# Second expert site: rows scattered to expert slots by chunks inside the linear attention, tiles loaded by plain transfers

## The chip, the cores and the metric

One core of one Trainium2 chip runs one kernel. The metric is device microseconds (us) of one launch. Five engines run their own instruction streams and meet at semaphores: PE (matrix products, into PSUM banks), ACT (activations), DVE (vector operations), POOL (vector operations and the issue of indirect DMAs) and SP (here only the issue of plain DMAs and the waits before them).

## The reference, cut to what matters

2048 tokens (8 sequences of 256) of 128 channels, float32, go through: a local-attention network of two layers, an attention with distance decay, the same local-attention network again, a mixture of experts, a linear attention, and the same mixture of experts again. The change is in the last two. The mixture is computed twice, each time on the normalised rows:

```python
x = x + 0.5 * _L1_ffn_ref(_layernorm(x), ...)          # first expert site
x = x + _L1_attn_ref(_layernorm(x), ...)               # linear attention, causal within 512 tokens
x = x + 0.5 * _L1_ffn_ref(_layernorm(x), ...)          # second expert site
# _L1_ffn_ref: D = 128, E = 12 experts, HR = 384, HS = 256, TAU = 1.5
ys = _geglu(xf @ Ws1 + bs1) @ Ws2 + bs2                # shared expert, all rows
logits = (xf @ Wr + br) / TAU
top_val, top_idx = jax.lax.top_k(logits, 2)            # two experts for each row
top_w = jax.nn.softmax(top_val)
yr = sum over the two picks of top_w * (_geglu(xf @ We1[e] + be1[e]) @ We2[e] + be2[e])
return ys + yr
```

## The kernel before, in words

**Tiles.** P = 128 rows are a tile, NT = 16 tiles are all rows, CT = 4 tiles are a chunk, NCH = 4 chunks. X holds the stream, U its normalised rows, uT those transposed. Two picks for each of 2048 rows are 4096 pairs. Sorted by expert and padded to whole tiles they fill at most NXT = 32 + 12 = 44 expert tiles of 128 rows, and the kernel always runs 44. Each stage below has its own stream on each engine (`la_pe`, `mx_dve` and so on), written out by hand, and semaphores are the only other order.

**Stages in order.** Local attention (site 0), decay attention, local attention (site 1), first expert site (`mx_*`, k0 = 0), linear attention (`la_*`), second expert site (`mx_*`, k0 = 1), final sum (`fin_*`). Before the decay attention, after it and around the linear attention stands `phase_end` (L313 to L319): each of PE, ACT, DVE and POOL executes a drain (L315) and then waits for the drains of the other three. SP does not take part.

**Linear attention.** The loop of `la_pe` over i handles chunk i at several depths: `out_proj(i-1)`, `x_turned(i-2)` (transposes of the newly normalised U, L2338), `sums(i)`, `scores(i+1)`, `o_turn(i)` and `logits(i-3)`, the router's product (L2345), whose result for all 16 tiles lies in one bank and is announced once. `la_dve` runs `gated`, `masked`, `result`, `features`, `divided` and `normed` (L2461, makes U) in that order, and `la_pool` computes the power of the variance for each chunk (L2554, L2556).

**Routing, in `mx_dve`.** Both sites do the same, for all 16 tiles at once after the phase end: scaled logits, the two largest and their indices, one-hot masks, weights by a power on POOL (L2193). PE counts rows by expert (`counts`). DVE forms prefix sums, the expert of each of the 44 tiles (`tef`, written as whole numbers to `te` by POOL, L2197), and a place for each pair. One-hot rings (24 of 32 by DVE at L2070, 8 by POOL at L2202) and 32 small products of PE (L1822) invert the places into two tables, `inv_u[0]` (which row each place reads) and `inv_u[1]` (where each place's result goes). Beside it PE and ACT compute the hidden layer of the shared expert (L1786, L1913).

**The expert loop.** For tile n: POOL gathers 128 rows of `u_rows` (a copy of U in DRAM, stored by SP at L2229) by `inv_u[0]` into one of XG = 8 buffers (L2182). PE transposes them (L1833), ACT copies that to xT (L1921), PE multiplies by We1 of the expert (12 instructions, L1845), ACT and DVE form the gated product (L1929, L2105), PE multiplies by We2 (6 instructions, L1859), ACT copies (L1936) and POOL scatters 128 rows to `y_rows` by `inv_u[1]` (L2188). POOL's order is gather(n), scatter(n - 12). SP loads We1 (384 KB) for each tile into one of four buffers once the first product of tile n - 4 has been issued and is done (L2236). It first reads the expert's number from `te` into a register (`expert`, L1777: a TENSOR_LOAD, a FUSED_REGOPS, a SEQ_ASSERT). The product of tile n+1 and the transposition of tile n+2 alternate in `group`. After the last scatter SP loads `y_rows` back, and DVE, ACT and POOL add to X.

Of the kernel before, what the change touches and what calls it, by code (L numbers as in the profile page):

```python
# [16 lines left out]
P = 128  # L17
# [23 lines left out]

V_BE1, V_BS1, V_B1, V_LG, V_LB, V_QKVB, V_LQKVB, V_LGATE, V_LNG, V_LNB, V_N = (
# [11 lines left out]
r_tab h_ld n_gps n_gate n_kps n_k n_neg n_exp n_kf n_qps n_qf n_vps n_v n_att n_am n_num n_den n_rec n_o  # L54
# [68 lines left out]
def build(nc, a, out):  # L123
    with ExitStack() as ctx:
# [177 lines left out]
        ndr = sb("ndr", [P, 2, CT])  # L302

        u_rows = nc.dram_tensor("u_rows", [NT * P, D], F32, kind="Internal").ap()
        y_rows = nc.dram_tensor("y_rows", [2 * NT * P + NXT * P, D], F32, kind="Internal").ap()
# [107 lines left out]
        def constants_pool(pool):  # L415
            pool.memset(ones[:, :], 1.0)
            pool.memset(wts[:, :, E:E + 1], 1.0)
            pool.memset(wts[:, :, E + 1:32], 0.0)
            pool.memset(ebase[:, :], float(np.e))
# [1327 lines left out]
        def sh_up(g):  # L1747
            return B[1 + 2 * g], B[2 + 2 * g]
# [21 lines left out]

        LD_X = (s.ld_x0, s.ld_x1, s.ld_x2, s.ld_x3, s.ld_x4, s.ld_x5, s.ld_x6, s.ld_x7)

# [6 lines left out]
        def mx_pe(pe, k0):  # L1779
            kc, base = k0 * NCH, k0 * NXT  # L1780

            def up(c, g):
                if c:
                    pe.wait_ge(s.s_a, 2 * (kc + c - 1) + g + 1)
                for half in range(2):
                    m = pe.matmul(sh_up(g)[half][:, :], ws1[:, (2 * half + g) * P:(2 * half + g + 1) * P],  # L1786
# [31 lines left out]
            def ring(m):  # L1818
                pe.wait_ge(s.inv_b, k0 * oh_dve(2 * NT) + oh_dve(m + 1))
                if oh_pool(m + 1):  # L1820
# [7 lines left out]
            def x_turn(i, o, q):  # L1828
                n, buf = 8 * i + 4 * o + q, 4 * o + q
                pe.wait_ge(LD_X[buf], 16 * (x_loads(k0, buf) + i + 1))  # L1830
# [47 lines left out]

            up(0, 0)
            up(0, 1)  # L1880
            up(1, 0)
            counts()
# [3 lines left out]
            weights_turn()  # L1886
# [5 lines left out]
            pe.wait_ge(s.r_pool, r_pools(k0) + 2)  # L1892
            pe.wait_ge(s.r_tab, 2 * k0 + 1)
            x_turn(0, 0, 0)
            x_turn(0, 0, 1)
            for i in range(OCT):
                group(i, 0)
                group(i, 1)
# [9 lines left out]
        def mx_act(act, k0):  # L1908
            kc, base = k0 * NCH, k0 * NXT

            def hidden(c, g):
                act.wait_ge(s.s_up, 2 * (kc + c) + g + 1)
                act.activation(acts[:, c, g, :], sh_up(g)[1][:, :], ACT.Gelu, bias=vec[:, V_BS1 + 2 + g:V_BS1 + 3 + g])  # L1913
                act.activation(sh_a[:, c, g, :], sh_up(g)[0][:, :], ACT.Identity, bias=vec[:, V_BS1 + g:V_BS1 + g + 1])\
# [17 lines left out]
            def y_out(n):  # L1932
                act.wait_ge(s.x_dn, base + n + 1)
                if n + k0 * NXT > 3:
                    act.wait_ge((s.st_y0, s.st_y1, s.st_y2, s.st_y3)[n % 4], 16 * (NXG * k0 + n // 4))
# [3 lines left out]
            for c in range(NCH):  # L1939
                for g in range(2):  # L1940
                    hidden(c, g)
                if c == 2:
                    act.wait_ge(s.r_wps, k0 + 1)
                    act.activation(wT[:, :], W_BANK[:, :], ACT.Copy).then_inc(s.r_wT, 1)
            act.wait_ge(s.r_pool, r_pools(k0) + 2)
            x_out(0)
            x_out(1)
            for n in range(NXT + 2):
# [7 lines left out]
        R_PLACES = 34  # L1956
        R_STEPS = 43
        R_TILES = 27

        def mx_dve(dve, k0, coef):  # L1960
            kc, base = k0 * NCH, k0 * NXT
            taken = [k0 * R_STEPS]
# [28 lines left out]
            dve.wait_ge(s.r_lg, k0 + 1)  # L1991
            done_(dve.tensor_tensor(lg, RING_LG.rearrange("p (t e) -> p t e", e=E), tiles_bc(br_row[:, :]), ALU.add))
            own()
            done_(dve.tensor_scalar(lg, lg, 1.0 / TAU, None, ALU.mult))
            own()
            for t in range(NT):
                m = dve.max(top[:, t, :], lg[:, t, :])
            done_(m)
            own()
            dve.tensor_tensor(rw[:, :, 0], top[:, :, 1], top[:, :, 0], ALU.subtract).then_inc(s.r_m12, 1)  # L2000
            for t in range(NT):
                m = dve.max_index(idx[:, t, :], top[:, t, :], lg[:, t, :])
            done_(m)
            own()
            done_(dve.tensor_copy(idf[:, :, :], idx[:, :, 0:2]))
            own()
            for n in range(2):
                m = dve.tensor_tensor(oh[n], tiles_bc(iota[:, 0:E]), experts_bc(idf[:, :, n]), ALU.is_equal)
            done_(m)
            own()  # L2010
            dve.tensor_tensor(both, oh[0], oh[1], ALU.add).then_inc(s.r_both, 1)

            dve.wait_ge(s.r_pool, r_pools(k0) + 1)
            done_(dve.tensor_scalar(rw[:, :, 0], rw[:, :, 1], 1.0, None, ALU.add))
            own()
            done_(dve.reciprocal(rw[:, :, 2], rw[:, :, 0]))
            own()
            done_(dve.tensor_tensor(rw[:, :, 3], rw[:, :, 1], rw[:, :, 2], ALU.mult))
            own()
            done_(dve.tensor_tensor(wtmp, oh[0], experts_bc(rw[:, :, 2]), ALU.mult))  # L2020
            done_(dve.tensor_tensor(wts[:, :, 0:E], oh[1], experts_bc(rw[:, :, 3]), ALU.mult))
            own()
            dve.tensor_tensor(wts[:, :, 0:E], wts[:, :, 0:E], wtmp, ALU.add).then_inc(s.r_w, 1)

            dve.wait_ge(s.r_cum, k0 + 1)
            done_(dve.tensor_copy(tot, RING_CUM[:, 256:256 + NT * E].rearrange("p (t e) -> p t e", e=E)))
            incl = prefix([tot, pre0, pre1], NT, lambda v, a_, b_: v[:, a_:b_, :])
            own()

            done_(dve.tensor_tensor(need, bc(incl[:, NT - 1, :].unsqueeze(2), [P, E, NT]),  # L2030
                                    bc(iota[:, E + NXT:E + NXT + NT].unsqueeze(1), [P, E, NT]), ALU.is_gt))
            own()
            done_(dve.tensor_reduce(ntile[:, :], need, AX_X, ALU.add))
            ends = prefix([ntile[:, :], etile[:, 0, :], etile[:, 1, :]], E, lambda v, a_, b_: v[:, a_:b_])
            done_(dve.tensor_tensor(place, incl, tot, ALU.subtract))
            own()
            done_(dve.tensor_tensor(ecmp[:, :, :], bc(ends.unsqueeze(1), [P, NXT, E]),
                                    bc(iota[:, E:E + NXT].unsqueeze(2), [P, NXT, E]), ALU.is_le))
            done_(dve.tensor_tensor(place, place, RING_CUM[:, 0:NT * E].rearrange("p (t e) -> p t e", e=E), ALU.add))
            done_(dve.tensor_tensor(ntile[:, :], ends, ntile[:, :], ALU.subtract))  # L2040
            own()
            done_(dve.tensor_reduce(tef[:, 0, :], ecmp[:, :, :], AX_X, ALU.add))
            assert taken[0] == k0 * R_STEPS + R_TILES, taken
            done_(dve.scalar_tensor_tensor(place, tiles_bc(ntile[:, :]), float(P), place, ALU.mult, ALU.add))
# [16 lines left out]
            assert taken[0] == k0 * R_STEPS + R_PLACES, taken  # L2061

            for m in range(2 * NT):
# [4 lines left out]
                if m % 8 in OH_POOL:  # L2068
# [14 lines left out]
            dve.tensor_copy(inv_u[:, 0, :], inv[:, 3, :]).then_inc(s.r_tab, 1)  # L2083
# [589 lines left out]
```

## Time and profile before

| | us |
|---|---|
| three timed runs | 1384.06, 1385.63, 1387.5 (median 1385.63) |
| the profiled execution | 1376.06 |
| its span, first to last instruction | 1374.3 |
| second expert site, from the phase end to the last product by We2 | 1183.0 to 1348.9 |
| mean granted TensorE clock | 0.955 of full |

Starts are us from the span's start, and durations are us. A row of the timeline merges equal instructions that follow each other: "x12" is twelve, and the second number runs from the start of the first to the end of the last. In brackets stands how long the engine was idle before and what released it. "PEclk" is the granted clock of PE as a share of full speed.

### The profile page before, as it was taken

How to read it: one execution, taken by the hardware profiler on the slowest of the kernel's cores; microseconds unless marked ns; L12 is line 12 of the kernel's file. 1: busy time of each engine (PE TensorE's matmuls, PEld its weight loads, DVE VectorE, ACT ScalarE, POOL GpSimd, SP SyncE). 2: the span in 40 equal slices, each digit the busy share in tenths (PEclk: the TensorE clock that was granted, in tenths of full speed). 3: DMA queues.
4: the chain of work that ended last, by engine and by line, in shares of the span. 5: the costliest groups of instructions: out<-in, count | busy, mean ns of one | idle time of the engine just before them, and what ended most of it. 6: DMA issues, size and time to landing. Idle time of an engine off the chain costs nothing.

```text
span 1374.3 us, 36568 instructions
## 1 busy us (share of the span) xinstructions
PE 1173.4 (85%) x12741; PEld 878.2 (64%) x12742; DVE 929.1 (68%) x2485; ACT 847.7 (62%) x2486; POOL 798.1 (58%) x712
## 2 busy tenths in 40 slices
PE   5899898998879999799989899898787858768784
PEld 2667675766745555467668566685687836457773
DVE  6988669986846777688866988688332367633233
ACT  3999768998435555489985899843243524313343
POOL 6788348884654352388744878443666532266653
PEclk9999999999989999999999999998899989879998
DMA  7011100111000000001110001132365520135564
GB/s 220 18 25 25 28 15 13 28 26 28 15 2 3 4 3 3 2 10 30 26 28 17 9 21 25 35 78 77 109 182 160 173 69 0 49 108 168 169 189 118
DMA packets 70226, 79.26 MB, mean 58 GB/s; under 512 B 25191, under 2 KB 50598, under 8 KB 69926
## 3 DMA queue, kind: packets, MB, share of 16 engines
q1 hardware_dynamic: 64421, 65.49, 17.2%
q0 software_dynamic: 5632, 11.55, 3.0%
q8 instruction: 100, 1.64, 0.5%
q14 instruction: 73, 0.59, 0.1%
HBM read 55.52 MB, written 8.91 MB: 47 GB/s over the span
## 4 chain that ended last, share of the span: by engine, by line
PE 33%; DVE 7%; ACT 6%; issue 4%; DMA 4%; POOL 2%; POOLq 1%; SPq 1%; another core or an unknown queue 1%; ACTq 0%; DVEq 0%
PE bank L1845 10%; PE bank L1859 4%; ACT pB L791 3%; PE bank L912 3%; DMA arena<-arena 2%; PE bank L633 1%; PE bank L924 1%; PE bank L596 1%; PE bank L541 1%; PE bank L555 1%; DVE mx L717 1%; PE bank L547 1%; POOL arena L2202 1%; PE bank L1786 1%; PE bank L1833 1%
## 5 line engine op out<-in xcount | busy, mean ns | idle before, releaser
L2105 DVE SCALAR_TENSOR_TENSOR act_b<-bank,vec,gl 128x128 f32<-128x128 f32 x264 | 76.8, 345 | 185.9 <-PE bank L1845 94.9
L860 POOL TENSOR_TENSOR rn<-ss,mhalf 128x16 f32<-128x16 f32 x64 | 187.8, 2934 | 6.7
L1929 ACT ACTIVATE gl<-bank,vec 128x128 f32<-128x128 f32 x264 | 77.9, 366 | 127.3 <-PE bank L1845 101.6
L1845 PE MATMUL bank<-arena 128*128 128x128 f32 x1056 | 141.3, 286 | 3.3 <-DVE act_b L2105 2.2
L1845 PEld LDWEIGHTS bank<-arena 128*128 128x128 f32 x1056 | 131.6, 200 | 10.1 <-issue 5.8
L2182 POOL DMA_INDIRECT arena<-u_rows,inv_u x88 | 87.0, 988 | 69.7 <-remote 33.3
L791 ACT ACTIVATE pA<-bank,nb,rn 128x128 f32<-128x128 f32 x256 | 113.7, 485 | 3.1 <-DVE nb L722 3.1
L791 ACT ACTIVATE pB<-bank,nb,rn 128x128 f32<-128x128 f32 x256 | 113.4, 477 | 1.7 <-DVE nb L722 1.7
L2188 POOL DMA_INDIRECT y_rows<-stg,inv_u x88 | 87.6, 996 | 42.9 <-ACT stg L1936 22.7
L846 POOL TENSOR_TENSOR arena<-arena 128x512 f32<-128x512 f32 x64 | 81.7, 1276 | 46.2 <-DVE nb L722 35.4
L853 POOL TENSOR_TENSOR arena<-arena 128x512 f32<-128x512 f32 x64 | 81.4, 1272 | 43.0 <-DVE arena L685 16.4
L1605 DVE TENSOR_REDUCE act_b<-bank 128x2 f32<-128x512 f32 x128 | 79.6, 685 | 32.9 <-PE bank L1487 32.9
L717 DVE TENSOR_REDUCE mx<-bank 128x4 f32<-128x512 f32 x128 | 82.4, 686 | 25.6 <-PE bank L596 25.6
L683 DVE TENSOR_TENSOR arena<-bank,arena 128x512 f32<-128x512 f32 x128 | 87.6, 684 | 14.5 <-ACT arena L758 13.3
L772 ACT ACTIVATE pT<-bank 128x512 f32<-128x512 f32 x128 | 77.2, 603 | 23.5 <-PE bank L608 20.5
L758 ACT ACTIVATE arena<-bank 128x512 f32<-128x512 f32 x128 | 77.9, 611 | 18.5 <-PE bank L541 11.1
L912 PE MATMUL bank<-hT,arena 128*128 128x256 f32 (+1 forms) x384 | 89.2, 382 | 0.0
L685 DVE TENSOR_TENSOR arena<-bank,arena 128x512 f32<-128x512 f32 x128 | 87.1, 681 | 0.0
L633 PE MATMUL bank<-pT,arena 128*64 128x64 f32 (+1 forms) x1536 | 71.9, 242 | 14.7 <-DMA arena<-arena 13.5
L1075 POOL TENSOR_SCALAR rs<-mv 128x2 f32<-128x2 f32 x48 | 10.9, 227 | 125.7 <-DVE mv L974 125.7
L780 ACT ACTIVATE arena<-bank 128x512 f32<-128x512 f32 x128 | 78.6, 614 | 8.6 <-PE bank L571 4.9
L1859 PE MATMUL bank<-arena,act_b 128*128 x528 | 76.1, 280 | 1.8 <-issue 1.8
(335 smaller groups left out, 3140.8 us busy)
## 6 DMA issues: line engine op xcount, KB each, us to landing
arena<-in_L_ffn_We SPq DMA_DIRECT2D x88, 384.0 KB
arena<-arena SPq DMA_DIRECT2D x64, 128.0 KB, 2.3
arena<-in_L_ffn_We SPq DMA_DIRECT2D x3, 768.0 KB, 7.2
arena<-U SPq DMA_DIRECT2D x32, 64.0 KB
u_rows<-U SPq DMA_DIRECT2D x2, 1024.0 KB, 6.0
U<-y_rows SPq DMA_DIRECT2D x8, 256.0 KB, 4.4
uT<-y_rows SPq DMA_DIRECT2D x8, 256.0 KB, 4.6
arena<-U SPq DMA_DIRECT2D x32, 63.5 KB
```

The source lines that it names most:

```text
L633: m = pe.matmul(BO[64 * x:64 * x + 64, cols], v[:, h * LD:(h + 1) * LD], pT[x][:, cols], start=True, stop=True)
L683: dve.tensor_tensor(heads(rab[:, 2 * k, :]), heads(bank[:, :]), bc(rtab[:, l, 2 * k, q % 2, :].unsqueeze(1), [P, LH, LD]), ALU.mult)
L685: dve.tensor_tensor(rab[:, 2 * k + 1, :].rearrange("p (h a d) -> p h a d", h=LH, a=2), flipped(bank[:, :]), bc(rtab[:, l, 2 * k + 1, q % 2 ...
L717: dve.tensor_reduce(mx8[:, par, x, :], BS[x][:, :].rearrange("p (u k) -> p u k", u=4), AX_X, ALU.max, negate=True)\
L791: m = act.activation(pr[:, u * P:(u + 1) * P], BS[x][:, u * P:(u + 1) * P], ACT.Exp, bias=nb8[:, par, x, u:u + 1], scale=rn[:, q % 4, 0, 2 ...
L846: pool.tensor_tensor(kadd[:, :], rab[:, 2, :], rab[:, 3, :], ALU.add).then_inc(s.kadd_ready, 1)
L860: pool.tensor_tensor(rn[:, q % 4, :, :], ss[:, 1, :].rearrange("p (a h) -> p a h", a=2), mhalf[:, :].rearrange("p (a h) -> p a h", a=2), A ...
L912: m = pe.matmul(MG[c][0:n, g * SEQ:(g + 1) * SEQ], w1[:, g * HID + h0:g * HID + h0 + n], hT2[:, :], start=True, stop=True)
L1845: m = pe.matmul(bank[q % 2][:, j * P:(j + 1) * P], we1[q][:, half * HR + j * P:half * HR + (j + 1) * P], xT[:, q, :], start=True, stop=True)
L1859: m = pe.matmul(XY[q % 2][:, 0:D], XACT[q][:, j * P:(j + 1) * P], we2[:, bass.ds(e * HR + j * D, D)], start=(j == 0), stop=(j == 2))
L2182: pool.indirect_dma_start(xg[:, n % XG, :], None, u_rows[:, :], bass.IndirectOffsetOnAxis(ap=inv_u[:, 0, n:n + 1], axis=0))\
L2188: pool.indirect_dma_start(y_rows[:, :], bass.IndirectOffsetOnAxis(ap=inv_u[:, 1, n:n + 1], axis=0), yb[:, n % 4, :], None)\
```

## The change

Only the second expert site and what leads to it are changed; the first keeps its gathers.

1. **Blank slots.** A DRAM tensor `x_slots` of 12 x 16 + 32 = 224 blocks of 128 rows (14.7 MB) is set to zero by seven plain DMAs of SP, issued between the transfers of site 0 and those of site 1. Each expert owns 16 blocks.
2. **Routing by chunks.** Logits of chunk c are computed one iteration of `la_pe` earlier than before, in a bank of their own. DVE picks experts for the chunk (`chunk_picks`), PE counts it (`chunk_counts`), DVE adds the running totals and has the slot of each pair (`chunk_slots`). Logits, counts and slots share one PSUM bank, so the logits of chunk c wait until the counts of chunk c - 1 have been read. Chunks 0, 1 and 2 are done in the linear attention and chunk 3 at the head of `mx_*`.
3. **Scatter of rows.** POOL writes each tile of U twice, to its slots, by an indirect DMA each (`row_out`): 32 in all. Eight (chunk 0) are in `la_pool`, four of them ahead of the power of chunk 3. The other 24 are at the head of `mx_pool`, with `te` computed after the 20th.
4. **The loop.** POOL's 44 gathers and the store of U go. SP loads the 44 tiles (64 KB each) by a plain DMA from a block number in a register, which takes a second read of `te` and a read of `sbase_u`. The first four follow the first four loads of We1 and wait for all rows to be written. The others follow the load of We1 of the same tile.
5. **Tables.** The places are still inverted, but only for the scatter of results. All 32 one-hot rings are made by DVE. The power and the weights come after them, and PE's transposition of the weights after the first two transpositions of the loop.

```diff
+        def blank_slots(sp):                       # between site_sync(sp, 0) and site_sync(sp, 1)
+            w = SLOT_BLOCKS // N_BLANK
+            for n in range(N_BLANK):
+                sp.dma_start(x_slots[n * w:(n + 1) * w, :, :].rearrange("b p d -> p b d"),
+                             bc(blank[:, :].unsqueeze(1), [P, w, D])).then_inc(s.stored, 16)
...
             if k0:
+                for c in (1, 2):
+                    for t in range(c * CT, (c + 1) * CT):
+                        for k in range(2):
+                            row_out(pool, t, k, LA_EVENT(c) + 7)
+                for t in range(NT - CT, NT):
+                    for k in range(2):
+                        row_out(pool, t, k, r_base(1) + 7)
+                    if t == NT - CT + 1:
+                        names()
+                power()
+                pool.wait_ge(s.r_self, r_base(k0) + R_SCATTER[k0])
+                for n in range(NXT):
+                    scatter(n)
+                return
...
+            def x_rows_in(n):                      # in mx_sync
+                e = expert(sp, n)
+                first = sp.value_load(sbase_u[0:1, bass.ds(e, 1)], min_val=0, max_val=(E - 1) * SLOT_E)
+                if not n:
+                    for sem in ST_Y:
+                        sp.wait_ge(sem, 16 * (NXG + ROWS_OUT))
+                if n >= 4:
+                    sp.wait_ge(s.x_ps, base + n - 3)
+                sp.dma_start(xg[:, n % XG, :], x_slots[bass.ds(first + n, 1), :, :].rearrange("o p d -> p (o d)"))\
+                    .then_inc(GAT[n % 4], 16)
...
                 sp.dma_start(we1[n % WB], a["L1_ffn_We1"][bass.ds(e, 1), :, :].rearrange("o k n -> k (o n)"))\
                     .then_inc((s.ld_e0, s.ld_e1, s.ld_e2, s.ld_e3)[n % WB], 16)
+                if k0 and n == WB - 1:
+                    for m in range(WB):
+                        x_rows_in(m)
+                elif k0 and n >= WB:
+                    x_rows_in(n)
...
             def logits(c):                         # in la_pe
                 pe.wait_ge(s.uT_ready, LA_T + NCH + c + 1)
-                pe.wait_ge(s.n_qf, NCH)
+                if c:
+                    pe.wait_ge(s.r_read, 2 * c)
+                else:
+                    pe.wait_ge(s.n_k, NCH)
...
-            for i in range(-1, NCH + 3):
+            for i in range(-1, NCH + 2):
...
+                if has(i - 3) and i - 3 < NCH - 1:
+                    chunk_counts(pe, i - 3)
                 if has(i):
                     o_turn(i)
-                if has(i - 3):
-                    logits(i - 3)
+                if has(i - 2):
+                    logits(i - 2)
...
                 if has(i):                         # in la_dve
                     divided(i)
+                if i == NCH:
+                    chunk_slots(dve, 1, LA_EVENT(1) + 4)
                 if has(i - 1):
                     normed(i - 1, 1)
+                if i == NCH - 2:
+                    chunk_picks(dve, 0, LA_EVENT(0))
+                if i == NCH - 1:
+                    chunk_slots(dve, 0, LA_EVENT(0) + 4)
+                    chunk_picks(dve, 1, LA_EVENT(1))
+                if i == NCH:
+                    chunk_picks(dve, 2, LA_EVENT(2))
+            chunk_slots(dve, 2, LA_EVENT(2) + 4)
...
+                if c == NCH - 1:                   # in la_pool
+                    pool.wait_ge(s.stored, 16 * (N_BLANK + 1))
+                    for t in range(CT):
+                        row_out(pool, t, t % 2, LA_EVENT(0) + 7)
                 power(c, 1)
+            for t in range(CT):
+                row_out(pool, t, 1 - t % 2, LA_EVENT(0) + 7)
             phase_end(pool, "pool", ph)
```

The new functions `row_out` (one wait, one indirect DMA of 128 rows from U to `x_slots`), `chunk_counts` (5 products on at most 48 columns), `chunk_picks` (13 DVE operations on 4 tiles) and `chunk_slots` (7 DVE operations) are called as shown.

## Rows read from the trace of the kernel before

**Rows 1.** The page: busy time and share of the span of each engine.

```profile
PE 1173.4 (85%) x12741; PEld 878.2 (64%) x12742; DVE 929.1 (68%) x2485; ACT 847.7 (62%) x2486; POOL 798.1 (58%) x712
```

**Rows 2.** Timeline of POOL, second site: expert numbers, steady loop, last scatter.

```profile
1197.56 0.43 POOL L2197 CAST te<-tef 128x44 uint32<-128x44 f32 x1
...
1273.59 0.97 POOL L2182 DMA_INDIRECT arena<-u_rows,inv_u  x1 [1.35 <-remote]
1274.87 0.99 POOL L2188 DMA_INDIRECT y_rows<-stg,inv_u  x1 [0.30 <-issue]
...
1279.82 0.97 POOL L2182 DMA_INDIRECT arena<-u_rows,inv_u  x1 [1.39 <-remote]
...
1350.54 0.97 POOL L2188 DMA_INDIRECT y_rows<-stg,inv_u  x1 [0.30 <-issue]
```

**Rows 3.** Timeline of PE: first and last transposition, two of the last tiles, end.

```profile
1212.62 0.45 PE L1833 MATMUL bank<-ident_sb,arena 128*128 128x128 f32 x1 [5.21 <-DMA arena<-u_rows,inv_u]
...
1332.62 1.50 PE L1845 MATMUL bank<-arena 128*128 128x128 f32 x12
...
1334.74 1.50 PE L1845 MATMUL bank<-arena 128*128 128x128 f32 x12
...
1343.11 0.27 PE L1833 MATMUL bank<-ident_sb,arena 128*128 128x128 f32 x1
...
1346.57 2.34 PE L1859 MATMUL bank<-arena,act_b 128*128 x18
```

**Rows 4.** SP's instructions at L1777, L2236, window 1198 to 1203: ns min/median/max, first/last start.

```profile
L1777 SPq TENSOR_LOAD <-te x4: 273/277/283, 1198.0 to 1201.7; - x4
...
L2236 SPq DMA_DIRECT2D arena<-in_L_ffn_We x4: 333/348/358, 1198.7 to 1202.4; - x4
```

**Rows 5.** The same for the window 1250 to 1328, POOL gathering and scattering.

```profile
L2236 SPq DMA_DIRECT2D arena<-in_L_ffn_We x25: 5/113/715, 1252.3 to 1326.8; - x25
...
L1777 SPq FUSED_REGOPS  x25: 16/152/717, 1250.2 to 1324.6; - x25
```

**Rows 6.** The same for the window 1334 to 1341, POOL only scattering.

```profile
L2236 SPq DMA_DIRECT2D arena<-in_L_ffn_We x3: 333/333/333, 1334.9 to 1339.1; - x3
```

**Rows 7.** Waits of SP's queue, 1250 to 1330: us in total, times, longest.

```profile
SPq L1777 <- PE bank L1845: 21.0, 9, 3.3
SPq L1777 <- remote: 8.1, 4, 2.6
```

**Rows 8.** Timeline of all engines around the phase end.

```profile
1174.51 1.01 POOL L2556 TENSOR_TENSOR rs<-rs,mhalf 128x4 f32<-128x4 f32 x1
...
1177.63 3.43 PE L2345 MATMUL bank<-wr,uT 128*128 128x12 f32 x16
...
1183.03 0.36 DVE L1992 TENSOR_TENSOR pA<-bank,br_row 128x192 f32<-128x192 f32 x1 [6.37 <-POOLq L315]
```

**Rows 9.** Drains at L315, window 1170 to 1184 (ns min/median/max).

```profile
L315 POOLq DRAIN  x1: 8324/8324/8324, 1174.5 to 1174.5; - x1
```

**Rows 10.** Timeline of DVE: masks and result of chunk 3, router, last rings.

```profile
1164.04 0.55 DVE L2491 TENSOR_TENSOR sm<-bank,causal_sb 128x384 f32<-128x384 f32 x1
...
1172.13 0.69 DVE L2517 TENSOR_TENSOR X<-bank,X 128x512 f32<-128x512 f32 x1 [1.64 <-PE bank L2329]
...
1183.72 1.25 DVE L1997 MAX8 top<-pA 128x8 f32<-128x12 f32 x16
...
1205.24 1.42 DVE L2070 TENSOR_SCALAR arena<-iota,posh,code_sb 128x128 f16<-128x128 f16 x6
```

**Rows 11.** One stretch: busy us (count) of PE, PEld, DVE, ACT, POOL; PEclk, DMA share, GB/s.

```profile
406.00:576.00 170.00, 154.13 (x3629) 95.61 (x3630) 117.35 (x237) 88.27 (x214) 61.35 (x41) 0.99 0.01 3
```

**Rows 12.** DMA issues of the page: KB each, us to landing.

```profile
arena<-arena SPq DMA_DIRECT2D x64, 128.0 KB, 2.3
...
u_rows<-U SPq DMA_DIRECT2D x2, 1024.0 KB, 6.0
```

**Rows 13.** Timeline of SP's queue: the first load back of results.

```profile
1352.86 0.39 SPq L2245 DMA_DIRECT2D U<-y_rows  x1
```

More of the change, by code:

```diff
@@ L302, in build @@
         ndr = sb("ndr", [P, 2, CT])
+        blank = sb("blank", [P, D])
+        run = sb("run", [P, E])
+        rank2 = sb("rank2", [P, 2, CT, E])
+        slotf = sb("slotf", [P, 2, CT])
+        slot_u = sb("slot_u", [P, 2, NT], U32)
+        sbase = sb("sbase", [P, E])
+        sbase_u = sb("sbase_u", [P, E], U32)
         u_rows = nc.dram_tensor("u_rows", [NT * P, D], F32, kind="Internal").ap()
+        x_slots = nc.dram_tensor("x_slots", [SLOT_BLOCKS, P, D], F32, kind="Internal").ap()
         y_rows = nc.dram_tensor("y_rows", [2 * NT * P + NXT * P, D], F32, kind="Internal").ap()
@@ L1881, in mx_pe @@
             up(1, 0)
-            counts()
+            if not k0:
+                counts()
             up(1, 1)
@@ L2001, in mx_dve @@
[L2001 to L2011, printed above, removed]
@@ L2045, in mx_dve @@
+            if k0:
+                chunk_picks(dve, NCH - 1, taken[0])
+                dve.wait_ge(s.r_self, taken[0] + 4)
+                dve.tensor_tensor(rw[:, :, 0], top[:, :, 1], top[:, :, 0], ALU.subtract).then_inc(s.r_m12, 1)
+                chunk_slots(dve, NCH - 1, taken[0] + 4)
+                taken[0] += 7
+                tables()
+            else:
+                first_picks()
+                softmax()
+                first_tables()
             own()
@@ new lines, in chunk_picks, with after @@
+        def chunk_picks(dve, c, event):
+            ts = slice(c * CT, (c + 1) * CT)
+            steps = itertools.count(event + 1)
+            def after(m):
+                m.then_inc(s.r_self, 1)
+                dve.wait_ge(s.r_self, next(steps))
+            dve.wait_ge(s.r_lg, c + 2)
+            dve.scalar_tensor_tensor(lg[:, ts, :], LA_LG.rearrange("p (t e) -> p t e", e=E)[:, ts, :], 1.0 / TAU,
+                                     bc(br_row[:, :].unsqueeze(1), [P, CT, E]), ALU.mult, ALU.add)\
+                .then_inc(s.r_read, 1)
+            dve.wait_ge(s.r_read, 2 * c + 1)
+            for t in range(ts.start, ts.stop):
+                m = dve.max(top[:, t, :], lg[:, t, :])
+            after(m)
+            for t in range(ts.start, ts.stop):
+                m = dve.max_index(idx[:, t, :], top[:, t, :], lg[:, t, :])
+            after(m)
+            after(dve.tensor_copy(idf[:, ts, :], idx[:, ts, 0:2]))
+            for k in range(2):
+                m = dve.tensor_tensor(oh[k][:, ts, :], bc(iota[:, 0:E].unsqueeze(1), [P, CT, E]),
+                                      bc(idf[:, ts, k].unsqueeze(2), [P, CT, E]), ALU.is_equal)
+            after(m)
+            dve.tensor_tensor(both[:, ts, :], oh[0][:, ts, :], oh[1][:, ts, :], ALU.add).then_inc(s.r_both, 1)
```

278 lines of the change are left out of this document (193 added, 85 removed).

## The prediction

> **What bounds the kernel now.** I read the page first. PE is busy for 85% of the span [rows 1], but the change touches only the last 250 us, so I went to the timelines of that stretch. From the phase end at 1183.0 [rows 8] the second site takes 29.6 us to the first transposition at 1212.6 and another 136.3 us to the end of the last product by We2 at 1348.9 [rows 3], 165.9 us in all.
>
> The loop has 44 tiles. In its steady part POOL issues gather, scatter, gather, scatter every 6.23 us (1273.59 to 1279.82): four indirect DMAs at 1.28 us each (0.97 to 0.99 busy and 0.30 between) and one extra wait of about 1.1 us [rows 2]. That is 3.11 us a tile. Once the gathers have run out, the same PE work repeats every 2.12 us (1332.62 to 1334.74) [rows 3]. So POOL's queue bounds the loop by 1.0 us a tile, and the change takes half of that queue's work away. It gives that work to SP, so SP's queue must be priced.
>
> SP spends one read of `te` and one DMA on each tile. Over the first four loads the starts of the DMAs go from 1198.7 to 1202.4, 1.23 us each, of which 0.7 us lies ahead of the DMA (1198.0 to 1198.7) and 0.5 us from there on [rows 4]. While POOL gathers and scatters SP is much slower: simple register instructions take up to 0.72 us [rows 5], and from 80 us for 26 tiles only 29.1 us are waits [rows 7], so one load occupies SP for (80 - 29.1) / 26 = 1.96 us. With scatters alone SP's DMA instruction is back at 0.33 us [rows 6].
>
> **The loop after the change.** Each tile costs SP its old 1.23 us, then `x_rows_in`: a second read of `te` (0.7), a read of `sbase_u` at an address from a register (another 0.7, as it is the same kind of read), and a DMA (0.5), together 1.9 us. That makes 3.1 us a tile. The bounds: 2.85 if the reads and address steps cost 0.6 each and the load 1.1, and 5.0 if SP stays as slow as beside gathers (3.1 x 1.96 / 1.23). I take 3.1, since scatters alone leave SP fast [rows 6]. Then the loop leaves a POOL bound of 3.11 us for an SP bound of 3.1 us and nothing is won, although POOL (1.28 us a tile) and PE (2.12) would both allow more.
>
> Here a rule of the Trainium skill speaks the other way. Its page "DMA: Bandwidth & Descriptors", section "SWDGE vs HWDGE vs iDMA", says that DMAs issued by SP have their descriptors made in hardware, with less setup than those that POOL's software writes. By that alone the loop would fall to PE's 2.12 us; this is my rival B. The trace agrees in part: SP's DMA instruction takes 0.35 us against POOL's 0.97 [rows 2, 4]. But the register reads around it cost more than it does.
>
> **The head of the second site.** Call the phase end P. POOL's first work is 16 row scatters for chunks 1 and 2, four for chunk 3, the two small operations for `te` (0.95 us, twice the 0.43 of its cast and a gap), and four more scatters. At 1.28 us a scatter [rows 2] that is 24 x 1.28 + 0.95 = 31.7 us. `te` is ready at P + 26.6, against 1198.0, which is P + 15.0, now. From the start of a scatter to SP's next instruction behind it now pass 2.3 us (1350.54 to 1352.86) [rows 2, 13], so all rows are in DRAM at about P + 33. The four We1 loads are issued between P + 26.6 and then, slowed by POOL, and I set the first tile load at P + 34. DVE is not what is late: picks and slots of chunk 3 (four of 16 tiles, then small operations), tables, places and 32 rings at 0.24 each [rows 10] end near P + 22, and PE's 32 ring products near P + 26. The power and the weights come behind the rows, at about P + 36, and are hidden by the first tile's own 4 us from transposition to gating.
>
> The next three tile loads follow at 1.9 us, to P + 39.7, and 40 more at 3.1 us, to P + 163.7. A small plain load lands in 2.3 us [rows 12], so the last transposition is at P + 166.0. From there to the end of the last product it is 1343.11 to 1348.91 today [rows 3], 5.8 us. Sum: P + 171.8, against P + 165.9 now: **+5.9 us**.
>
> **The linear attention.** `chunk_picks` handles 4 of 16 tiles. Its four MAX8 are a quarter of 1.25 us [rows 10]. With the four index searches, four small operations on 48 columns at 0.2 to 0.3 us and a wait between steps I estimate 2.0 us for it, `chunk_slots` about 1.4, `chunk_counts` about 1. `chunk_picks(0)` comes ahead of the masks of chunk 3, which DVE starts at 1164.04 without an idle gap [rows 10]: 2.0 to 2.4 us later. `chunk_slots(0)` and `chunk_picks(1)` come ahead of the result of chunk 3. DVE is idle for 1.64 us there [rows 10], and `logits(1)` must wait for the slots and holds up the output product: another 2.7 us. The power of chunk 3 waits behind four scatters on POOL (5.1 us), about as late as the result: 0.3 us. U is then 5 us later, and POOL has four scatters left. Behind U the chain picks, counts, slots, logits(3) takes about 9 us to the phase end, where transposition, copy and 16 products (the last end at 1181.1) and the drains took 6.3 [rows 8]. By this chain P moves by 7 to 8 us.
>
> There is a second chain. Today the phase end is released by POOL's drain: POOL's last operation ends at 1175.5 and its drain, 8.32 us from 1174.5 [rows 8, 9], ends at 1182.8, 7.3 us after POOL had nothing left. It is the only drain with indirect DMAs behind it. If it costs that again after the last scatter, P = power's end (1180.5) + 5.1 + 7.3 = 1192.9, **+9.9 us**. If it only waited for something that goes (the store of U runs in those same microseconds), P moves by 7. I take 9.9.
>
> **The blanks.** 14.7 MB at the rate of the store of U (1 MB in 6.0 us [rows 12]) are 84 us of full DMA, begun when SP has issued the last transfer of site 0. They fall into the end of that site and the decay attention, where SP has little to issue; the compute of 406 to 576 us uses 1% of the DMA engines [rows 11], so the transfers are hidden unless instruction fetches wait behind them. Bounds 0 and +6; I take 1. SP's row stores and `u_rows` in the first site wait for them without effect 400 us later.
>
> **Sum.** +5.9 + 9.9 + 1 = +16.8 us. The profiled execution goes from 1376.1 to 1392.9 us. It is 9.6 us below the median of the timed runs, so on that scale 1385.6 + 16.8 = **1402.4 us**, 1.2% slower. Own range: loop from 2.85 to 3.5 us a tile (-10, +16), head and attention from -7 to +5, blanks to +6: 1388 to 1426.
>
> **Rivals.**
> - *B, PE becomes the bound, faster.* SP's reads overlap or cost less than I think. From a first transposition at P + 36.3, 44 tiles at 2.12 us, 5.8 us for two of the shared expert's turns in the loop and 6 us at start and end make P + 147.4, so 18.5 us less than P + 165.9, and with +10.9 for attention and blanks -7.6: 1378 us; if attention and head are milder too, 1370. It decides from SP's time per tile: below 2.6 us the sum turns negative. For it: POOL is half free. Against it: no row has a read and a DMA on SP under 1.1 us.
> - *C, SP stays slow.* If even single scatters stretch its instructions to 0.7 us, as beside gathers [rows 5], a tile costs 4 to 5 us: 40 x 0.9 to 1.9 more, 1438 to 1478 us. Against it: [rows 6].
> - *D, a wash.* SP at 2.85 us, a short drain and a milder attention: +16.8 - 10 - 3 - 2 gives 1387.
> - *E, the change does not do what it says:* it would if rows did not land before loads; the waits exclude it, chance 0.
>
> **Chances.** Forecast 0.60, B 0.12, C 0.13, D 0.15. A measurement of this kernel tells 0.3%, 4 us, from no change: faster takes B and a little of D (0.14), same most of D and a little of the forecast (0.13), slower the rest (0.73). The range of 8 in 10, with the near parts of B and C: 1378 to 1440.
>
> **What would show it.** Right: first transposition about 36 us behind the phase end; SP without waits on PE and tiles 3.0 to 3.2 us apart; POOL idle between scatters; a POOL drain of several us that ends the attention 7 to 10 us later. Wrong: tiles 2.1 to 2.6 us apart (B), SP instructions of 0.7 us through the loop (C), DVE or PE as the last releaser of the first transposition, or PE idle on instruction fetch while the blanks are written.

## The result, and the profile after

The changed kernel took 1394.07 us (median of 7 runs, 1385.4 to 1400.34), the kernel before 1384.06 us in the same comparison (7 runs, 1381.8 to 1388.61): a ratio of 1.0066, 95% interval [1.0044, 1.0088]. That is slower by 10.0 us, where 16.8 were forecast. The profiled execution of the changed kernel took 1391.53 us (span 1389.6), 15.5 us more than the profiled one of before. The two differences, 10.0 and 15.5, are not the same thing: each profile is one execution, that of before 8.0 us below its median of seven, that of the changed kernel 2.5 us below its own. Much of what follows is about that gap of 5.5 us.

By stages, first-chip profiles, us (each edge is a row of the timelines, as [rows 3, 8] for before):

| stage | before | after | change | forecast |
|---|---|---|---|---|
| up to the end of the first site's last product | 1100.9 | 1100.6 | -0.3 | +1 |
| from there to the phase end | 82.1 | 93.3 | +11.2 | +9.9 |
| head: phase end to first transposition | 29.6 | 41.2 | +11.6 | +6.7 |
| loop: first transposition to end of last product | 136.3 | 130.2 | -6.1 | -0.8 |
| tail | 25.4 | 24.3 | -1.1 | 0 |

The page of the changed kernel, against [rows 1] and [rows 12]: POOL loses 22 us of work and PE gains 12, and the tile loads land in 1.9 us.

```profile
PE 1185.2 (85%) x12777; PEld 885.9 (64%) x12778; DVE 936.9 (67%) x2529; ACT 852.6 (61%) x2486; POOL 776.4 (56%) x693
...
x_slots<-blank SPq DMA_DIRECT2D x7, 2048.0 KB, 17.8
arena<-arena SPq DMA_DIRECT2D x64, 128.0 KB, 2.3
arena<-x_slots SPq DMA_DIRECT2D x44, 64.0 KB, 1.9
```

The phase end, from the timeline of all engines and the drains at L327 (count, ns min/median/max, start). POOL's last scatter ends at 1185.8, and its drain ends 8.0 us later and releases DVE, as in [rows 8, 9] but 10.9 us later on the clock.

```profile
1184.83 0.95 POOL L2758 DMA_INDIRECT x_slots<-U,slot_u  x1 [0.30 <-issue]
...
1193.94 0.21 DVE L2405 SCALAR_TENSOR_TENSOR pA<-bank,br_row 128x48 f32<-128x48 f32 x1 [6.27 <-POOLq L327]
```

```profile
L327 POOLq DRAIN  x1: 14039/14039/14039, 1179.7 to 1179.7; - x1
L327 ACTq DRAIN  x1: 626/626/626, 1183.2 to 1183.2; - x1
L327 PEldq DRAIN  x1: 1872/1872/1872, 1187.3 to 1187.3; - x1
```

The head, from the timelines of POOL, SP and PE. `te` is cast at P + 26.3 (forecast P + 26.6), the last scatter starts at P + 30.6, but the first tile load starts at P + 38.7 (forecast P + 34) and the first transposition at P + 41.2. SP's four We1 loads ahead of it stretch over 6.5 us (third fence: ns min/median/max, first and last start). The two steps at which SP waits for the scatters then pass at 1232.4 and 1232.5, in 28 ns at most.

```profile
1220.23 0.22 POOL L2284 CAST te<-tef 128x44 uint32<-128x44 f32 x1
...
1224.51 0.98 POOL L2758 DMA_INDIRECT x_slots<-U,slot_u  x1 [0.30 <-issue]
```

```profile
1232.65 5.58 SPq L2333 DMA_DIRECT2D arena<-x_slots  x4
```

```profile
L2354 SPq DMA_DIRECT2D arena<-in_L_ffn_We x4: 338/352/698, 1224.3 to 1230.8; - x4
```

```profile
1235.10 0.45 PE L1865 MATMUL bank<-ident_sb,arena 128*128 128x128 f32 x1 [5.29 <-DMA arena<-x_slots]
```

The loop, from SP's instructions between 1250 and 1350 and from the waits between 1240 and 1360 (us in total, times, longest). SP alternates the two loads and waits for PE only 4.2 us in all. POOL now waits 92 us for something to scatter, and PE waits for tiles. From the fifth load of We1 at 1240.57 to the last at 1354.78 are 39 tiles: 2.93 us each.

```profile
L1806 SPq TENSOR_LOAD <-te x69: 13/269/416, 1249.9 to 1349.4; - x69
...
L2327 SPq TENSOR_LOAD <-sbase_u x34: 234/277/343, 1250.6 to 1347.2; - x34
...
L2333 SPq DMA_DIRECT2D arena<-x_slots x34: 14/338/731, 1251.4 to 1348.4; - x34
...
L2354 SPq DMA_DIRECT2D arena<-in_L_ffn_We x34: 16/338/347, 1252.8 to 1349.0; - x34
```

```profile
POOL y_rows L2271 <- ACT stg L1974: 92.3, 40, 16.0
...
PE bank L1865 <- DMA arena<-x_slots: 15.5, 23, 1.9
```

```profile
SPq L1806 <- PE bank L1877: 4.2, 11, 1.6
```

### The profile page after: what moved, and what is told of

It reads as the page before. It is cut to its first block, busy times and chain, and to the rows that moved or that the text cites. A ratio compares the mean times of both kernels' runs of the same rounds, so it can differ in the third digit from the quotient of the medians.

```text
span 1389.6 us, 37088 instructions
## 1 busy us (share of the span) xinstructions
PE 1185.2 (85%) x12777; PEld 885.9 (64%) x12778; DVE 936.9 (67%) x2529; ACT 852.6 (61%) x2486; POOL 776.4 (56%) x693
## 4 chain that ended last, share of the span: by engine, by line
PE 27%; issue 11%; SPq 5%; DMA 5%; ACT 4%; DVE 4%; POOL 1%; ACTq 0%; DVEq 0%; POOLq 0%; another core or an unknown queue 0%
PE bank L1877 7%; PE bank L925 2%; PE bank L1891 2%; ACT pB L804 2%; DMA arena<-x_slots 2%; DMA arena<-arena 2%; SPq L1806 2%; PE bank L646 2%; PE bank L568 1%; PE bank L554 1%; PE bank L937 1%; PE bank L609 1%; PE bank L560 1%; PE bank L621 1%; PE bank L658 1%
## 5 line engine op out<-in xcount | busy, mean ns | idle before, releaser
L1877 PEld LDWEIGHTS bank<-arena 128*128 128x128 f32 x1056 | 132.0, 200 | 9.2 <-issue 5.6
L696 DVE TENSOR_TENSOR arena<-bank,arena 128x512 f32<-128x512 f32 x128 | 87.5, 684 | 12.9 <-ACT arena L771 11.9
L1088 POOL TENSOR_SCALAR rs<-mv 128x2 f32<-128x2 f32 x48 | 10.9, 226 | 126.4 <-DVE mv L987 126.4
L718 DVE TENSOR_REDUCE ss<-arena 128x16 f32<-128x1024 f32 x64 | 77.3, 1208 | 0.0
```

The costliest lines, as they stand in the source:

```text
L696: dve.tensor_tensor(heads(rab[:, 2 * k, :]), heads(bank[:, :]), bc(rtab[:, l, 2 * k, q % 2, :].unsqueeze(1), [P, LH, LD]), ALU.mult)
L1877: m = pe.matmul(bank[q % 2][:, j * P:(j + 1) * P], we1[q][:, half * HR + j * P:half * HR + (j + 1) * P], xT[:, q, :], start=True, stop=True)
```

## The experiments

Sixteen runs in four groups, each group on one chip, and no chip twice. On all four of these chips the kernel before took 1328 us (medians 1328.1 to 1328.2), 56 us less than on the chip of the result. So these runs show two things at once, what each edit does and what differs between chips.

### The kernel before on other chips

No edit; four profiles on three chips.

> The kernel before, unchanged, for a second trace of it. Its first profiled execution took 1376.1 us, its seven timed ones 1381.8 to 1388.6. If executions differ by that in the expert loops, a second trace lies 5 to 10 us above the first, and the surplus is in the stretch between the first transposition and the last product of one or both sites. If the first trace was ordinary, the second has the same stage lengths within 1 us.

> The kernel before once more, for its two gather loops. Theory: what differs between chips and executions lies in these two loops alone (134.3 and 136.3 us in the first profile, 111.7 and 110.3 on the fast chip, other stages within 1 us). On a fast chip both loops take 110 to 112 us again; on a slow one both take 130 us or more. Rival: other stages differ too, by over 2 us.

Measured: 1330.99, 1328.04, 1325.32 and 1323.88 us. What sets them apart from the first chip lies in the two gather loops: 111.7 and 110.3 us, 110.6 and 109.8, 112.0 and 109.9, 110.5 and 110.5, where the first chip had 134.3 and 136.3. The stage from the first loop to the phase end (80.2 to 82.3), the head (29.3 to 29.5) and the tail (25.2 to 25.9) are as on the first chip. POOL's timeline on one of them:

```profile
1241.21 0.97 POOL L2182 DMA_INDIRECT arena<-u_rows,inv_u  x1 [0.30 <-issue]
1242.48 0.99 POOL L2188 DMA_INDIRECT y_rows<-stg,inv_u  x1 [0.31 <-issue]
1243.78 0.97 POOL L2182 DMA_INDIRECT arena<-u_rows,inv_u  x1 [0.30 <-issue]
1245.05 0.99 POOL L2188 DMA_INDIRECT y_rows<-stg,inv_u  x1 [0.30 <-issue]
1246.34 0.97 POOL L2182 DMA_INDIRECT arena<-u_rows,inv_u  x1 [0.30 <-issue]
```

The waits of 1.35 us ahead of gathers in [rows 2] are gone, and a tile takes 2.57 us of POOL. SP's stretched instructions are gone too, to be read against [rows 5]: on the first chip the DMA of We1 took 5 to 715 ns and the register step up to 717.

```profile
L2236 SPq DMA_DIRECT2D arena<-in_L_ffn_We x33: 337/338/347, 1210.3 to 1289.4; - x33
```

```profile
L1777 SPq FUSED_REGOPS  x33: 152/152/159, 1209.9 to 1289.0; - x33
```

> The kernel before. Theory: its time less 1106 us is the sum of its two gather loops (1376.06 us with 134.3 + 136.3, 1330.99 us with 111.7 + 110.3), on a chip of either sort. Rival: another stage moves by over 2 us.

> The kernel before once more on the same chip: its gather loops against those of before_fourth. Theory: on a slow chip they differ by some us between executions and all other stages by under 1 us; on a fast chip both loops are within 2 us of 111 us.

Time less both loops is 1105.5 us for the first chip's profile and 1109.0, 1107.6, 1103.4 and 1102.9 for these. The rule holds within 4 us, but the rival has a part in it: the first transposition of the first site starts anywhere from 964.2 to 971.7 us in these four profiles (966.7 on the first chip). So what differs between the first chip and the others lies in the loops, and what differs among these four executions lies ahead of them: their two loops together take 220.4 to 222.1 us.

### The changed kernel on the same chips

> The changed kernel once more. The gather loop of the kernel before took 134 to 136 us in the first profile and 110 to 112 us on the faster chip. Theory: the changed second loop is paced by SyncE's register reads, 2.93 us a tile, and these don't depend on the chip, so its second loop takes 130 to 132 us wherever it runs. Phase end and head cost +12 and +9.5 over the kernel before, the tail -1.5. Where the kernel before takes 1328 us this makes 1328 + 21 + 12 + 9.5 - 1.5 = 1369 us (ratio 1.03); where it takes 1384, about 1394. Rival: what slows the gather loop on the first chip slows every loop there, and the changed loop would be as much faster on the fast chip (110 us, 1348 us in all, ratio 1.015).

> The changed kernel once more. Theory: its second loop takes 130 to 133 us on any chip, while its first, still with gathers, follows the chip (110 or 134 us). Rival: the second loop follows the chip too.

> The changed kernel. Theory: +38 to +44 us (ratio 1.029 to 1.033) where the kernel before takes 1328 us; +10 us (1.007) where it takes 1384 us, with a second loop of 130 to 133 us in both. Rival: the ratio is 1.03 on a slow chip as well.

Measured: 1366.79 us, ratio 1.0287 [1.0254, 1.032]; a single execution of 1372.11 us beside 1328.2; and 1367.18 us, ratio 1.0296 [1.0266, 1.0327]. So there the change costs 39 us. Second loop: 133.1, 132.1 and 130.8 us, against 130.2 on the first chip, while the first loop, which still gathers, went from 135.0 to 110.4, 111.4 and 112.1. The loop of plain loads does not care which chip it runs on; the gather loop does. The means of four profiles of before and three of after, other chips: to the phase end 81.2 to 92.7 (+11.5), head 29.4 to 38.1 (+8.7), loop 110.1 to 132.0 (+21.9), tail 25.6 to 23.9 (-1.7).

### The loop: SP's register reads

The tile load takes the register of the We1 load (`one_read_less`); every tile from block n at a fixed address, so that the tiles hold other rows than they should (`fixed_blocks`); one more read, unused (`more_reads`):

```
-                e = expert(sp, n)                      # one_read_less: e is handed in
 
-                e = expert(sp, n)                      # fixed_blocks
-                first = sp.value_load(sbase_u[0:1, bass.ds(e, 1)], ...)
-                sp.dma_start(xg[:, n % XG, :], x_slots[bass.ds(first + n, 1), :, :]...)
+                sp.dma_start(xg[:, n % XG, :], x_slots[n:n + 1, :, :]...)
 
+                expert(sp, n)                          # more_reads
```

> The kernel after, but x_rows_in keeps the expert number that the load of We1 has read, so SP reads two registers a tile from memory instead of three. Theory SP (SP's own instructions bound the loop): a tile takes 2.93 - 0.56 = 2.4 us, the 40 tiles behind the first four take 22 us less, and the kernel is about 20 us faster than the changed one, 1373 us. Rival DMA (the landing of 384 + 64 KB a tile bounds the loop): no change beyond 2 us. Rival PE: the same, PE is busy at 2.12 us a tile and could not go below that.

> The kernel after, but tile n is loaded from block n at a fixed address, so x_rows_in reads no register at all. Left out: the tiles are not those of their experts, so results are wrong in value while all sizes and counts of work stay. Theory SP: SP needs 1.1 + 0.4 = 1.6 us a tile, the loop falls to PE's 2.12 us a tile and the kernel is 25 to 30 us faster than the changed one, about 1366 us. Rival DMA: 448 KB a tile plus a 64 KB scatter cannot pass at 2.12 us (240 GB/s); then tiles stay above 2.5 us and PE waits for We1 or for the tile.

> One more read of the expert number into a register of SyncE for each tile load, used for nothing. Theory: the second loop is paced by SyncE's register reads at 0.56 us each: 2.93 + 0.56 = 3.49 us a tile, the second loop +22 to +25 us (130 to 154). Rival: the loop is paced by the landing of the tile or of We1, and a read beside it is hidden: +0 to +4 us.

| reads for each tile, SP | loop, us | We1 load to We1 load, us | time (before 1328) |
|---|---|---|---|
| 1 (fixed_blocks) | 110.8 | 2.44 | 1348.0, ratio 1.015 [1.0125, 1.0175] |
| 2 (one_read_less) | 116.5 | 2.56 | 1350.6, ratio 1.0164 [1.0143, 1.0186] |
| 3 (after_again) | 133.1 | 2.98 | 1366.8 |
| 4 (more_reads) | 153.3 | 3.49 | 1390.3 (one execution) |

From three reads to four a tile costs 0.51 us more, near the 0.56 expected of a read: SP is the bound. From two to one only 0.12 goes, so both expectations missed: 2.56 where 2.4 was expected, 2.44 where 2.12 was. There the loop has met PE. PE is busy for 84.3 of 90 us with two reads; in `fixed_blocks` it is busy for 82.1 of 85 us, at a granted clock of 1.00, and SP, no longer the bound, waits for PE's products 28.6 us (in the changed kernel 3.0 us in 100). The rival of that run, the landing of tiles, is out: it wanted more than 2.5 us a tile and a PE that waits, and PE waits for tiles 1.7 us in all. The 2.12 us are the expert's products alone; the loop also has the shared expert's products in it, 5.9 us of the 85. The window's row gives PE, PEld, DVE, ACT, POOL, granted clock, DMA share and GB/s:

```profile
1220.00:1305.00 85.00, 82.10 (x691) 78.14 (x690) 33.08 (x108) 46.32 (x171) 33.87 (x35) 1.00 0.73 214
```

```profile
SPq L1806 <- PE bank L1877: 28.6, 32, 3.5
```

PE is nearly as full in the gather loop of before on these chips (85.5 of 90 us in `before_again`). The profile of `one_read_less` is of its slowest execution by 7 us, 1360.4 us; `early_rows` below, with the same reads, has loops of 115.7 and 115.0 us. The timeline of SP's queue in `more_reads` shows the step directly: 2.29 us from We1 load to tile load (two `te` reads and one of `sbase_u`) and 1.10 from there on (one read), so 0.6 for each of the other two.

```profile
1280.44 0.33 SPq L2355 DMA_DIRECT2D arena<-in_L_ffn_We  x1
1282.73 0.33 SPq L2334 DMA_DIRECT2D arena<-x_slots  x1
1283.83 0.64 SPq L2355 DMA_DIRECT2D arena<-in_L_ffn_We  x1
1286.42 0.33 SPq L2334 DMA_DIRECT2D arena<-x_slots  x1
1287.53 0.33 SPq L2355 DMA_DIRECT2D arena<-in_L_ffn_We  x1
```

### The phase end: POOL's drain

```
         def la_pool(pool, ph):
+            pool.drain()
```

> The kernel after, with one more drain on POOL as the first instruction of the linear attention, where POOL waits for 8 us anyway. Theory (a drain costs about 0.083 us for each indirect DMA issued since the drain before it: 7.3 us for 88, 8.0 us for 96): the new drain takes 7.3 us in POOL's idle time, the one at the phase end about 0.7 us after POOL's last scatter instead of 8.0, and PE's chain ends the phase, 4 to 5 us earlier. Rival (a drain behind any indirect DMA costs 7 to 8 us whatever their number): the phase end does not move.

Measured: 1362.26 us, ratio 1.0247 [1.0224, 1.027]. The changed kernel itself, on other chips, has 1.0287 and 1.0296, so about 5 us go (from group to group, the kernel before stands within 0.1 us). The drains of this kernel and what releases DVE:

```profile
L327 POOLq DRAIN  x1: 7777/7777/7777, 1157.3 to 1157.3; - x1
...
L327 PEldq DRAIN  x1: 1863/1863/1863, 1165.5 to 1165.5; - x1
```

```profile
1167.53 0.21 DVE L2405 SCALAR_TENSOR_TENSOR pA<-bank,br_row 128x48 f32<-128x48 f32 x1 [1.65 <-PEq L327]
```

The drain ends at 1165.1, 1.7 us after the last scatter instead of 8.0, and PE's chain ends the phase: 87.5 us from the first loop instead of 92.7, 6.3 over before where I had 7 to 8 for that chain. So of the 11.5 us by which the phase end moved, the drain alone accounts for 5.2, and the chain of picks, counts, slots and logits for the rest. The same line in the kernel before:

> The kernel before with one more POOL drain as the first instruction of the linear attention. Theory: the drain at the phase end (8.3 us, begun at 1174.5 and ending 0.2 us before the next phase) falls to under 2 us, and the phase ends with PE's or DVE's own drain instead: 0 to -2 us in the phase end. Rival: the early drain (9.5 us) delays POOL's first powers of the linear attention and costs what it saves, or more: +1 to +5 us.

Measured: 1326.98 us, ratio 0.9998 [0.9983, 1.0014]: nothing. Its phase-end drain fell from 8.3 to 1.1 us, but PE's chain ends just behind it:

```profile
L315 POOLq DRAIN  x1: 1114/1114/1114, 1151.0 to 1151.0; - x1
```

The theory of `early_drain`, that a drain costs a little for each indirect DMA since the drain before it, has a second test that the traces hold. POOL's very last drain, with which the span ends, has 88 indirect DMAs since the one before it in the kernel before, 68 in the changed kernel and 60 in `fewer_scatters` (below):

```profile
L124 POOLq DRAIN  x1: 8676/8676/8676, 1365.3 to 1365.3; - x1
```

```profile
L128 POOLq DRAIN  x1: 7042/7042/7042, 1382.0 to 1382.0; - x1
```

```profile
L128 POOLq DRAIN  x1: 6389/6389/6389, 1347.5 to 1347.5; - x1
```

That is 1.63 us for 20 and 0.65 us for 8, 0.08 us each. It also explains the tail, which ends with this drain: the prediction had called the phase end's drain the only one with indirect DMAs behind it, and this is another. I had forecast 0 for the tail, and it got 1.1 us shorter on the first chip and 1.7 elsewhere.

### The head: 24 scatters

```
-                for c in (1, 2):
+                for c in (2,):
 ...
-        ROWS_OUT = 2 * NT // 4
+        ROWS_OUT = 2 * (NT - CT) // 4
```

> Leaves out the 8 scatters of chunk 1, so that block rows of that chunk stay blank. Theory: the head (phase end to first transposition, 38 to 41 us) is bound by POOL's 24 scatters at 1.27 us, so 8 fewer take 8 to 10 us off: 28 to 31 us, with the cast of the expert numbers 10 us earlier. Rival: the head is bound by VectorE's ranks and table (done 26 us after the phase end) with the load behind it, and only 2 to 4 us go: 35 to 38 us.

Measured in one execution: 1356.11 us; phase end (1172.55) to first transposition 27.7 us, against 38.1, so 10.4 us for 8 scatters (8 x 1.27 = 10.2). The theory holds: on this chip POOL's queue sets the head, and SP waits for the last scatters before its first tile load, 1.7 us here and 3.2 us in `after_again`. The run doesn't separate the scatters from the cast of `te`, which stands behind them in the same queue and starts SP's loads; both came 10 us earlier.

```profile
SPq L2330 <- DMA x_slots<-U,slot_u: 1.7, 1, 1.7
```

```profile
1200.24 0.45 PE L1865 MATMUL bank<-ident_sb,arena 128*128 128x128 f32 x1 [5.47 <-DMA arena<-x_slots]
```

### The blanks

> The kernel before with the seven blank transfers (14 MB into x_slots, issued by SyncE at the end of the second local attention) and nothing else of the change. Theory: hidden, the decay attention is not bound by transfers: 0 to +1 us. Rival: they delay SyncE's queue or the loads behind it: +3 to +6 us (the upper bound of the prediction).

Measured: 1326.84 us (10 runs), ratio 0.9984 [0.9971, 0.9997]. The blanks are hidden; for the small gain no row is shown.

### A better version

`early_rows` is `one_read_less` with the early drain, and:

```
-            phase_end(pool, "pool", ph)
+            pool.drain().then_inc(done["pool"], 1)
+            for t in range(CT, 2 * CT):
+                for k in range(2):
+                    row_out(pool, t, k, LA_EVENT(1) + 7)
+            ...                                        # waits for the others, as phase_end
```

with `names()` ahead of the last 8 scatters.

> The changed kernel with three edits together: the tile load reuses the register of the We1 load (one read less a tile), POOL drains once at the start of the linear attention, and the 8 scatters of chunk 1 are issued by POOL between its drain at the phase end and its wait for the others; the expert numbers are cast before the last 8 scatters. Theory: loop -15 us (131.7 to 116.5 measured for the register alone), phase end -6, head -3 to -5: 24 to 26 us under the changed kernel of the same call. That is 1343 to 1345 us where the kernel before takes 1328 (still +1.1%), and about 1369 where it takes 1384 (-1%). Rival: the parts overlap, the head is bound by VectorE's table instead, and the sum is -18 us or less.

> The version with one register read less, the early drain and the scatters of chunk 1 moved into POOL's wait at the phase end. Theory: +15 us over the kernel before where that takes 1328 us; on a chip where that takes 1384 us, -15 us or so (ratio 0.99). Rival: +15 us on both.

Measured: 1343.26 us, ratio 1.013 [1.0102, 1.0158], and 1341.29 us, ratio 1.0094 [1.0064, 1.0123]. It wins back 24 to 26 us of the change's 39, as expected, and is still slower than the kernel before. Loop 115.7 and 115.0 us, head 33.6 and 33.4. What is left over before is about 7.5 us to the phase end, 4 in the head and 5 in the loop, less the tail's 2. Whether it beats the kernel before on a chip like the first is not shown: none of the four is like it.

## Why the prediction was right and wrong

**The sign and the stages: right.** On the profiles of the first chip the sum was +16.8 and came out at +15.3. The attention (+9.9, measured +11.2) was well priced. The last scatter ended at 1185.8, where I had 1185.6, and the drain released the phase 8.0 us later for my 7.3; with an early drain it ended 1.7 us later. The drain is shown to end the phase, and to be worth 5.2 us of the shift. The blanks cost nothing (0 to +6 given, 1 taken). The bound of the changed loop was named rightly: SP's queue, with no wait on PE to speak of, shown by the step from 2 to 3 and 4 reads. The figure was 3.1 us and is 2.93, because a read of a value into a register costs SP 0.5 to 0.6 us, and not 0.7. The Trainium skill ("DMA: Bandwidth & Descriptors", section "SWDGE vs HWDGE vs iDMA") gives SP's DMAs the faster setup, and the trace agrees as far as that goes: the DMA instruction takes 0.34 us on SP and 0.97 on POOL. But with its reads the loaded tile takes 1.8 us of SP's queue, more than the 1.27 of the gather that it replaces.

**The head: mis-sized.** It was given +6.7 us and took +11.6 (+8.7 elsewhere). The step "the first tile load at P + 34" failed. POOL's part was exact (`te` P + 26.3, last scatter's start P + 30.6). But I let SP go on 2.3 us after a scatter's start, by the row of the last scatter of before [rows 13]; behind 24 scatters back to back SP's load comes 5.4 us after that start (1205.1 to 1210.5 in `after_again`), of which 3.2 us are a wait for the scatters. On the first chip it comes 8.1 us after, and not because of the scatters, for which SP does not wait there: between `te` at P + 26.5 and the first tile load SP took 12.2 us for four We1 loads and two reads, where I had 7.4. Its instructions, and DVE's, ran in steps of 0.7 us there. With the loop's -6.1 for -0.8 the two errors cancelled by luck: head and loop together +5.5, forecast +5.9.

**The time: wrong in the step from the profile to the timed median.** This is the step of the sum that failed. I added the whole sum to 1385.6, "on that scale", as if the 9.6 us by which the timed runs lay above the profiled one would stay. They can stay only if they lie outside what the change removes. Between the first chip and the others the kernel before differs in its two gather loops and nearly nowhere else, and the change takes one of the two away. If the executions on the first chip vary in the same place, half of 9.6 goes with it: 1385.6 + 16.8 - 4.8 = 1397.6, 0.25% from the measured 1394.07. That the spread between chips lies in these loops is shown. That the spread between the executions on the first chip does is inferred, since there is no second trace from there, and the four profiles of before from the other chips speak rather against it: there the spread lies ahead of the loops. So this account is one that fits, worked out after the result, and not one that is shown. What is shown is the size: 6.8 us of the sum did not arrive (16.8 forecast, 10.0 measured), 1.5 of them in the stages, where 15.3 came, and 5.3 in going from the two profiles to the medians; another 1.6 us of the 8.3 between 1402.4 and 1394.07 are the kernel before itself (1385.6 in three runs, 1384.06 in seven).

**A reading that looked right and was not.** This is the step of the mechanism that failed. I read "POOL's queue bounds the loop by 1.0 us a tile" from four indirect DMAs plus an extra wait of 1.1 us [rows 2]. The wait was not POOL's work: the profile gives its releaser as "remote", and for a few of these waits as PE's transposition, and on four other chips it does not occur, the loop takes 110 us, and the change costs 3% and not 0.7%. The rows for it stood in the prediction: instructions of SP at 0.72 us [rows 5] beside 0.33 elsewhere [rows 6]. I used them to price SP, and did not ask what the loop of before would be without them. By these rows POOL's own bound was 4 x 1.28 / 2 = 2.56 us a tile, and 40 tiles at that are 22 us less than 3.11, which is most of the 26 us found. What made the wait stays open.

**Rivals.** B (PE becomes the bound) is excluded at 2.93 us a tile. Its bound is real, and `fixed_blocks` reaches it at 2.44 us, but no gain comes with it on chips without the extra wait: that run is still 1.5% slower than the kernel before, and `one_read_less`, at 2.56 us a tile and so below the 2.6 at which I had the sum turn negative, 1.6%. B's terms were also added wrongly: 36.3 + 93.3 + 5.8 + 6 is 141.4 and not 147.4, which makes 1372 us and not 1378. C (SP stays slow beside single scatters) is out on every chip. Of D's three terms (1387 us) the drain was long and the attention not milder, and the faster SP came part of the way, 2.93 us a tile for its 2.85. Only the lowest of the seven runs reached its size; still, the median lies 7 us from it and 8 from the forecast. The terms of my own range give 1385 to 1428, and not 1388 to 1426; the result lies inside either.

## What to carry to other kernels

A load issued with computed addresses costs its queue the register reads too: count values read per iteration (here about 0.55 us each) before moving work from one queue to another, and reuse registers. A wait for which the profile names no engine of the kernel may belong to the chip, as it did here, so price a loop both with and without it; and a difference between a profile and the timed runs must be placed in a stage before it is carried over to a changed kernel. Here indirect DMAs put right ahead of a barrier paid the barrier's drain, and those put right behind it paid their issue time in full.

## What the runs showed of the hardware

- A POOL drain grew with the indirect DMAs issued since the drain before it. The last one took 8.68 us after 88, 7.04 after 68 and 6.39 after 60, 0.08 us each. At the phase end it ended 7.3 us after POOL's last work with 88 behind it, 8.0 with 96, 1.7 with 8 (`early_drain`), and took 1.1 us in all with none (`before_drain`). The early drain itself took 9.5 us for 88.
- On one chip of five, instructions ran in steps of 0.7 us in the stretches in which POOL issued indirect DMAs back to back: SP's register steps, VectorE's rings (0.31 us of work with 0.9 to 1.1 between, released by nothing), and some of PE's runs of twelve products (2.8 us in the chain of waits of before, 1.34 else). The two did not start and end together: in the head of the changed kernel the scatters run from 1195 to 1225 us, and VectorE's steps from 1212 to 1230. So the scatters may be a condition, and are not shown to be the cause. The four others show none of it: in their sixteen traces no register step of SP (FUSED_REGOPS, MOVE, SEQ_ASSERT) is over 0.2 us long, where the first chip has 76 such steps in the kernel before and 52 in the changed one. The timeline of DVE in the changed kernel on that chip:

```profile
1223.64 0.31 DVE L2148 TENSOR_SCALAR arena<-iota,posh,code_sb 128x128 f16<-128x128 f16 x1 [0.88 <-issue]
...
1225.76 0.32 DVE L2148 TENSOR_SCALAR arena<-iota,posh,code_sb 128x128 f16<-128x128 f16 x1 [1.09 <-issue]
1227.14 0.31 DVE L2148 TENSOR_SCALAR arena<-iota,posh,code_sb 128x128 f16<-128x128 f16 x1 [1.07 <-issue]
```

What makes that chip differ is open.
